# The last sums of a loop pass moved across the loop's branch in a graph network's edge loop

## The chip, the cores and the metric

One Trainium2 chip, one of its eight cores. The metric is the device time of one execution in microseconds, the median of the runs; the profile is of one further execution. All times below are in microseconds unless marked ns.

## What is computed

A graph network of three layers over 3125 nodes and 100000 undirected edges (each is used in both directions), 128 features a node and 16 an edge. A layer builds a message for every edge direction from the two end nodes and the edge, sums the messages at each receiving node, and updates the nodes. At the end stands a layer norm.

```python
def _L0_gnn_ref(nf, ef, src, dst, We1, We2, Wn1, Wn2):
    N, E, D, EF, L = (3125, 12500, 128, 16, 3)
    s2 = jnp.concatenate([src, dst])
    d2 = jnp.concatenate([dst, src])
    ef2 = jnp.concatenate([ef, ef], axis=0)
    h_prev = nf
    for l in range(L):
        e_in = jnp.concatenate([h_prev[s2], h_prev[d2], ef2], axis=-1)
        msg = jax.nn.leaky_relu(e_in @ We1[l]) @ We2[l]
        red = jax.ops.segment_sum(msg, d2, num_segments=N)
        n_in = jnp.concatenate([h_prev, red], axis=-1)
        out = jax.nn.leaky_relu(n_in @ Wn1[l]) @ Wn2[l]
        h_prev = out + h_prev
    return out
...
x = _layernorm(x + _L0_gnn_ref(x, edge_attr_16, src, dst, ...), axis=-1)
```

## The kernel before

**What is done once.** Edges are sorted into buckets by the pair of node blocks (of 128 nodes each; there are 25 blocks) that they join, and cut into tiles of 128 edges that lie in one bucket. For each tile two block numbers are kept, as byte offsets of the blocks: in the array `map_row`, of which a row holds 12 words, the offsets of the 6 tiles of two steps.

**The edge loop.** A step handles three tiles (`STEP`). TensorE does two things in it. *Gathers:* for each tile it multiplies the edge features by their weights (`features`, line 1446, one matmul) and adds the rows of the two end nodes, picked from a table of node features by one-hot matrices `gsel` (`gather`, line 1453, four matmuls, high and low halves). Tile 0 of a step goes to the accumulator `gath6`, a part of `sums`; tiles 1 and 2 go to `gath`. *Sums:* it adds the messages of three steps earlier (`LAG`) to the sums of their nodes (line 1514, 12 matmuls of 128x128, high and low halves, with one-hot matrices `ssel`). The place in `sums` is taken from the offsets.

Between these stand the other engines. ScalarE copies `gath6` to `msg` (line 837), then clears `gath6` (line 840), copies `gath` to `msg` (line 842), and makes the high half of the message of the step before (line 846). The vector engine applies the leaky relu (line 1179) and makes the low half (line 1199). SP issues the loads of `gsel`, `ssel` and the edge features a part (three steps) ahead; in layers 1 and 2 they come from memory, where layer 0 has put them.

**The waits of TensorE in a step**, in order, each on the semaphore named: the part's features and `gsel` (first step of a part alone); `x_set` of the step before (line 842 has emptied `gath`), ahead of the second tile; `ssel` of the part before and `mlo_set`, ahead of the third; and ahead of the sums `gath6_free` (line 840 has cleared `gath6`). `sum_done` is raised at the end of the sums; ScalarE waits for it at line 846 and SP ahead of its loads.

**The loops.** 12 steps are a turn (`STEPS`), and the number of turns, `live_n`, is found at run time. ScalarE, the vector engine and SP loop over 31 turns, of which those from `live_n` on are empty. TensorE loops over 16 passes of two turns, 24 steps: `with pe.If(it * 2 < live_n)` takes the first turn, and an inner `If` the second. Its code for a pass is written out, so that nothing but the loop's branch, two `If`s and the address arithmetic comes between steps. A hint for the branch is given with the loop (`hint_back_edge=True`).

**The offsets in registers.** In layers 1 and 2 TensorE loads a row of 12 words every second step (`next_row(q)`, called within `step` between gathers and sums). Rows that a pass leaves to the next go to the register sets `kept[2]`, `kept[1]` and `kept[0]` (rows 10, 11 and 12 of the pass: the last two rows of this pass, which the late sums still need, and the first of the next). Row 12 is loaded at step 23, the last of a pass, whole. Sums of a step read the row of three steps earlier.

**The end of a layer.** After its last sums TensorE runs the empty passes, leaves the loop, and in `node(l)` begins to multiply (line 1530) once ScalarE has read the sums out (line 852).

## Time and profile before

| | us |
|---|---|
| median of three runs | 3601.3 |
| lowest, highest of them | 3598.9, 3687.4 |
| the profiled execution, its time | 3590.8 |
| its span | 3589.1 |
| about 0 to 1215: sorting, tables | 1215 |
| about 1215 to 2010: edge loop of layer 0 | 795 |
| 2042.7 to 2774: edge loop of layer 1 | 731 |
| 2810.0 to 3541: edge loop of layer 2 | 731 |

The page gives, for one execution, the busy time of each engine and groups of instructions by line. PE is TensorE's matmuls and PEld its weight loads, which run beside them; DVE is the vector engine, ACT is ScalarE, SPq the queue from which SP issues DMAs. In a timeline a row is one instruction or a few like ones: start, duration, engine, line, what it writes and reads, how many, and in brackets how long the engine stood idle ahead of it and who ended that. "issue" in such brackets, or in the chain of waits, is time in which the engine waited for nothing that the profile shows. Ends of matmuls are modelled, so their starts are the safer mark.

### The profile page before, as it was taken

Reading aid. Unit: us, or ns where it says so; the run is one execution under the profiler, and the core shown is the slowest. Engines: PE = TensorE matmul, PEld = TensorE weight load, DVE = VectorE, ACT = ScalarE, POOL = GpSimd, SP = SyncE. Lnnn points to the kernel's source line nnn. Section 1 sums busy time; section 2 is a strip of 40 time slices with the busy share of each in tenths; the row PEclk is TensorE's granted clock in tenths of the full one; section 3 lists DMA queues with packets and bytes.
Section 4 is the critical chain, followed back from the end, with each engine's and each line's share of the span. In section 5 each row is a group of like instructions: output and inputs, shape, how many; then the busy total and the mean of one; then the engine's idle time right before and its main releaser. Section 6 shows DMA issues by size and latency. Waiting matters only on the chain.

```text
span 3589.1 us, 80534 instructions
## 1 busy us (share of the span) xinstructions
PE 2433.9 (68%) x26761; PEld 2105.1 (59%) x26762; DVE 2739.8 (76%) x3385; ACT 2060.4 (57%) x4138; POOL 799.9 (22%) x870
## 2 busy tenths in 40 slices
PE   5000000000004899999999999999999999999996
PEld 4000000000003678787887788888888788888885
DVE  8956565656554799999999877777777777777776
ACT  4000000000002677777877688888888788888885
POOL 0477777777774100000000100000000100000000
PEclk9555555555556999999999999999999999999998
DMA  8111111111112777777777455555555355555553
GB/s 251 46 45 44 34 45 33 45 32 45 30 22 82 239 245 255 256 251 251 253 253 247 169 195 187 189 194 194 190 185 194 120 189 187 193 195 192 185 192 126
DMA packets 227338, 563.52 MB, mean 157 GB/s; under 512 B 43272, under 2 KB 124238, under 8 KB 227182
## 3 DMA queue, kind: packets, MB, share of 16 engines
q1 hardware_dynamic: 199758, 547.80, 44.5%
q0 software_dynamic: 27552, 15.37, 2.3%
q8 instruction: 15, 0.25, 0.0%
q14 instruction: 13, 0.11, 0.0%
HBM read 413.11 MB, written 150.16 MB: 157 GB/s over the span
## 4 chain that ended last, share of the span: by engine, by line
PE 50%; POOL 19%; issue 15%; DVE 13%; SPq 1%; DMA 1%; ACT 1%; DVEq 0%; another core or an unknown queue 0%; ACTq 0%; POOLq 0%
POOL records L672 19%; PE gath L1453 18%; PE sums L1514 13%; PE sums L1453 9%; PE gath L1446 5%; DVE loop_buf L1199 3%; DVE big L1179 3%; PE sums L1446 2%; DVE loop_buf L1216 2%; DVE gsel L1183 2%; DVE table L1137 1%; DVE table L926 1%; PE sums L1530 0%; DMA nums_d<-numT 0%; PE sums L1531 0%
## 5 line engine op out<-in xcount | busy, mean ns | idle before, releaser
L1179 DVE SCALAR_TENSOR_TENSOR big<-big 128x768 f32<-128x768 f32 (+1 forms) x957 | 908.3, 949 | 372.9 <-ACT big L842 349.6
L1453 PE MATMUL gath<-table,gsel 128*128 x7488 | 1072.5, 273 | 0.0
L1199 DVE TENSOR_TENSOR loop_buf<-big,loop_buf 128x768 f16<-128x768 f32 x936 | 890.1, 951 | 0.0
L672 POOL DMA_INDIRECT records<-rec,rowi x784 | 751.4, 958 | 284.5 <-issue 247.3
L1514 PE MATMUL sums<-loop_buf 128*128 128x128 f16 x11232 | 780.3, 219 | 17.1 <-issue 14.1
L1453 PEld LDWEIGHTS gath<-table,gsel 128*128 128x128 f16 x7488 | 732.7, 98 | 83.8
L846 ACT ACTIVATE loop_buf<-big 128x768 f16<-128x768 f32 x936 | 781.4, 835 | 0.0
L842 ACT ACTIVATE big<-gath 128x512 f32<-128x512 f32 x936 | 559.1, 597 | 271.2 <-PE gath L1453 271.2
L1514 PEld LDWEIGHTS sums<-loop_buf 128*128 128x128 f16 x11232 | 649.8, 98 | 105.6 <-ACT sums L840 35.3
L1339 PE MATMUL sums<-table,fchunk 128*128 128x200 f16 x196 | 37.1, 365 | 877.1 <-DVE found L1031 864.7
L1453 PE MATMUL sums<-table,gsel 128*128 x3744 | 562.6, 273 | 14.2 <-DVE gsel L1183 14.2
L1339 PEld LDWEIGHTS sums<-table,fchunk 128*128 128x128 f16 x196 | 24.6, 136 | 889.3 <-issue 886.8
L782 ACT ACTIVATE rec<-big,sc_ef 128x448 f16 x28 | 18.7, 668 | 881.0 <-DMA records<-rec,rowi 881.0
L1446 PE MATMUL gath<-wst,fchunk 128*128 128x256 f16 x1872 | 510.8, 273 | 0.0
L837 ACT ACTIVATE big<-sums 128x256 f32<-128x256 f32 x936 | 352.3, 376 | 92.8 <-PE sums L1453 92.4
L1453 PEld LDWEIGHTS sums<-table,gsel 128*128 128x128 f16 x3744 | 361.3, 98 | 60.2 <-DVE gsel L1183 28.7
L840 ACT ACTIVATE sums<-iota 128x256 f32<-128x256 f16 x936 | 362.9, 388 | 29.6
L707 POOL TENSOR_SCALAR wcs<-wts,sc_w 128x128 f32<-128x128 f32 x2 | 1.2, 611 | 1581.8 <-DVE sc_w L1121 1581.8
L1446 PE MATMUL sums<-wst,fchunk 128*128 128x256 f16 x936 | 255.7, 273 | 37.3 <-issue 37.3
L1052 DVE SCALAR_TENSOR_TENSOR rowi<-rowb,rowc 128x28 int32<-128x28 int32 x28 | 5.3, 188 | 326.3 <-DMA records<-rec,rowi 326.0
L1446 PEld LDWEIGHTS gath<-wst,fchunk 128*128 128x128 f16 x1872 | 183.0, 98 | 31.7 <-issue 0.2
L1216 DVE TENSOR_TENSOR loop_buf<-numc,iota 128x768 f16<-128x768 f16 x312 | 172.0, 551 | 3.9 <-DMA ssel_d<-loop_buf 0.3
(196 smaller groups left out, 1651.3 us busy)
## 6 DMA issues: line engine op xcount, KB each, us to landing
gsel<-gsel_d SPq DMA_DIRECT2D x208, 576.0 KB, 3.7
loop_buf<-ssel_d SPq DMA_DIRECT2D x208, 576.0 KB, 5.1
numb<-nums_d SPq DMA_DIRECT2D x106, 576.0 KB, 4.6
gsel_d<-gsel SPq DMA_DIRECT2D x104, 576.0 KB, 5.5
ssel_d<-loop_buf SPq DMA_DIRECT2D x104, 576.0 KB, 6.4
fchunk<-feat_d SPq DMA_DIRECT2D x630, 80.0 KB, 4.5
loop_buf<-rows_d SPq DMA_DIRECT2D x28, 896.0 KB
records<-rec,rowi POOLq DMA_INDIRECT x784
```

Source lines behind the costliest of these rows:

```text
L672: pool.indirect_dma_start(out=records[:, :], out_offset=bass.IndirectOffsetOnAxis(ap=rowi[:, h, g:g + 1].bitcast(U32), axis=0), in_=rec[:, ...
L837: act.activation(msg[:, place, 0:2 * D], gath6, ACT.Copy).then_inc(x6_set, 1)
L840: act.activation(gath6, iota[:, 0:2 * D], ACT.Copy, scale=0.0).then_inc(gath6_free, 1)
L842: act.activation(msg[:, place, 2 * D:MSG], gath[:, :], ACT.Copy).then_inc(x_set, 1)
L846: act.activation(m_hi[:, (q - 1) % RING, :], msg[:, (q - 1) % RING, :], ACT.Copy)\
L1179: return dve.scalar_tensor_tensor(m, m, SLOPE, m, ALU.mult, ALU.max)
L1183: dve.tensor_scalar(gsel[:, h, :], numb[:, h, :], part[:, 0:1], None, ALU.is_equal).then_inc(gsel_set[h], DMA)
L1199: dve.tensor_tensor(m_lo[:, place, :], msg[:, place, :], m_hi[:, place, :], ALU.subtract)\
L1216: last = dve.tensor_tensor(ssel[:, t % SLOTS:t % SLOTS + STEP, :, :].rearrange("p t s (e w) -> p (t s) e w", w=2), numc[:, 2 * t:2 * (t + ...
L1446: pe.matmul(uv, fchunk[:, p % PARTS, pair * P:(pair + 1) * P], wst[:, side, :, :].rearrange("p s f -> p (s f)"), start=fresh, stop=False, ...
L1453: return pe.matmul(uv, gsel[:, h, (2 * tc + s) * P:(2 * tc + s + 1) * P], at[n], start=False, stop=n == 3, skip_group_check=True)
L1514: last = pe.matmul(sum_at[i, s], m[:, place, w0:w0 + D], ssel[:, ts, s, :], start=False, stop=False, skip_group_check=True)
```

## The change

`step` is parted into `gathers` and `add_sums`. In layers 1 and 2 the last step of a pass (q = 23) does its gathers alone, then comes the loop's branch. The sums of that step (`add_sums(-1, ...)`) stand at the head of the next pass, inside a new `pe.If(it > 0)`. For the pass behind the last live one there is a new `pe.Else()` of the outer `If`: when `it * 2 < live_n + 1`, it loads 8 words of the row that these sums need and does them there. Since `next_row(23)` is no longer called, row 12 is loaded in two pieces: 8 words at step 22, the other 4 at step 0 of the next pass. Layer 0 is as before, and so are all other engines.

```diff
--- before.py
+++ after.py
@@ -88,7 +88,8 @@
 LAG_LOADS = -(-LAG // LOAD_STEPS)
 STEP_WORDS = 2 * STEP
 LOAD_WORDS = LOAD_STEPS * STEP_WORDS
-assert STEPS % LOAD_STEPS == 0 and LOAD_WORDS % 4 == 0
+FIRST_WORDS = 8
+assert STEPS % LOAD_STEPS == 0 and LOAD_WORDS % 4 == 0 and STEP_WORDS <= FIRST_WORDS < LOAD_WORDS
 SLOPE = 0.01
 DEAD = 1000
 EXP_MASK = 0x7F800000
@@ -1457,15 +1458,13 @@
 
                 return [lowered(row(place, s, half)) for s, place in enumerate(places(t)) for half in range(2)]
 
-            def step(q, places, step0, turn, turn_n, before_sums):
+            def gathers(q, places, step0, turn, turn_n):
 
                 p = q // PART_STEPS
                 h = p % 2
                 t = STEP * q
                 first = q % PART_STEPS == 0
                 uv6, uv7 = gath6, (gath[:, 0:2 * D], gath[:, 2 * D:4 * D])
-                sum_at = {}
-
 
                 rows0 = gather_rows(places, t)
                 x_free = at_least(step0 + (q + AHEAD))
@@ -1481,7 +1480,6 @@
 
 
                 rows1 = gather_rows(places, t + 1)
-                free6 = at_least(step0 + (q + 1))
                 pe.wait_ge(x_set, x_free)
                 features(uv7[0], t + 1, p, True)
                 for n in range(4):
@@ -1498,7 +1496,11 @@
                     last = gather(uv7[1], rows2, t + 2, h, n)
                 last.then_inc(gath7_done, 1)
 
-
+            def add_sums(q, places, step0, before_sums):
+
+                t = STEP * q
+                sum_at = {}
+                free6 = at_least(step0 + (q + 1))
                 for i in range(STEP):
                     at = places(t + i - STEP * LAG)
                     for s in (1, 0):
@@ -1515,6 +1517,11 @@
                                              stop=False, skip_group_check=True)
                 last.then_inc(sum_done, 1)
 
+            def step(q, places, step0, turn, turn_n, before_sums):
+
+                gathers(q, places, step0, turn, turn_n)
+                add_sums(q, places, step0, before_sums)
+
             def load_words(first):
 
                 pe.reg_load(words, word_row[0:1, ds(first, WORDS)])
@@ -1587,9 +1594,9 @@
                 tables(l, l - 1)
                 pe.sem_inc(pe_go, 1)
 
-                def row_words(j, turn_n):
-
-                    return map_row[j % LOADS:j % LOADS + 1, ds((turn_n + 1 + j // LOADS) * LOAD_WORDS, LOAD_WORDS)]
+                def row_words(j, turn_n, first=0, count=LOAD_WORDS):
+
+                    return map_row[j % LOADS:j % LOADS + 1, ds((turn_n + 1 + j // LOADS) * LOAD_WORDS + first, count)]
 
                 def bounded(place):
 
@@ -1618,8 +1625,12 @@
                                     row_words(j, it * 2), engines=(mybir.EngineType.PE,),
                                     min_val=0, max_val=(NB - 1) * NODE_BYTES,
                                     skip_runtime_bounds_check_because="sums of the constant steps over the first buckets")
-                            elif q % LOAD_STEPS == LOAD_STEPS - 1:
+                            elif q % LOAD_STEPS == LOAD_STEPS - 1 and j < 2 * LOADS:
                                 keep_row(j, it * 2)
+                            elif q == 2 * STEPS - LOAD_STEPS:
+                                pe.reg_load(kept[0][0:FIRST_WORDS], row_words(2 * LOADS, it * 2, 0, FIRST_WORDS))
+                            elif q == 0:
+                                pe.reg_load(kept[0][FIRST_WORDS:], row_words(0, it * 2, FIRST_WORDS, LOAD_WORDS - FIRST_WORDS))
 
                         def places_at(t):
 
@@ -1628,14 +1639,30 @@
                                                        for r in kept[-j % (2 * LOADS)]]
                             return [bounded(place) for place in row_at[k:k + 2]]
 
+                        with pe.If(it > 0):
+                            add_sums(-1, places_at, step0, lambda q: None)
                         for q in range(STEPS):
                             step(q, places_at, step0, turn, l * live_n + it * 2, next_row)
                         with pe.If(it * 2 + 1 < live_n):
-                            for q in range(STEPS, 2 * STEPS):
+                            for q in range(STEPS, 2 * STEPS - 1):
                                 step(q, places_at, step0, turn, l * live_n + it * 2, next_row)
+                            gathers(2 * STEPS - 1, places_at, step0, turn, l * live_n + it * 2)
                         with pe.Else():
                             for j in range(-LAG_LOADS, 1):
                                 keep_row(j, 0)
+                    with pe.Else():
+                        with pe.If(it * 2 < live_n + 1):
+                            _, ended = nc.values_load_multi_w_load_instructions(
+                                row_words(-LAG_LOADS, it * 2, 0, FIRST_WORDS), engines=(mybir.EngineType.PE,),
+                                min_val=0, max_val=(NB - 1) * NODE_BYTES,
+                                skip_runtime_bounds_check_because="sums of the constant steps over the first buckets")
+
+                            def ended_at(t):
+
+                                k = 2 * t + LAG_LOADS * LOAD_WORDS
+                                return [bounded(place) for place in ended[k:k + 2]]
+
+                            add_sums(-1, ended_at, l * live_n * STEPS + it * (2 * STEPS), lambda q: None)
                 node(l)
 
             for n in range(YSTEPS):
```

## Rows read from the trace of the kernel before

**Rows 1.** The page: busy us of each engine, share of the span, instructions
```profile
PE 2433.9 (68%) x26761; PEld 2105.1 (59%) x26762; DVE 2739.8 (76%) x3385; ACT 2060.4 (57%) x4138; POOL 799.9 (22%) x870
```

**Rows 2.** The page's costliest groups: ScalarE's copy of gath6, whole span
```profile
L837 ACT ACTIVATE big<-sums 128x256 f32<-128x256 f32 x936 | 352.3, 376 | 92.8 <-PE sums L1453 92.4
```

**Rows 3.** Stretches, one pass: length, busy us by engine, TensorE clock, DMA share, GB/s
```profile
core 0: us, PE busy (x) PEld busy (x) DVE busy (x) ACT busy (x) POOL busy (x), PEclk, DMA share, GB/s
2380.88:2437.14 56.26, 55.55 (x648) 49.83 (x648) 43.83 (x49) 47.86 (x96) 0.00 (x0) 1.00 0.54 191
```

**Rows 4.** Chain of waits, layers 1 and 2: start, us, what
```profile
2098.73 0.79 issue
...
2717.77 0.71 issue
...
2865.55 0.71 issue
...
3484.45 0.71 issue
```

**Rows 5.** Timeline around the branch behind a pass of layer 1
```profile
2433.50 0.60 ACT L842 ACTIVATE big<-gath 128x512 f32<-128x512 f32 x1 [0.29 <-PE gath L1453]
...
2435.13 0.39 ACT L840 ACTIVATE sums<-iota 128x256 f32<-128x256 f16 x1
...
2435.57 0.69 PEld L1514 LDWEIGHTS sums<-loop_buf 128*128 128x128 f16 x12
...
2436.64 0.35 SPq L626 DMA_DIRECT2D gsel<-gsel_d  x1
2437.14 0.10 PEld L1446 LDWEIGHTS sums<-wst,fchunk 128*128 128x128 f16 x1 [0.88 <-issue]
2437.15 0.28 PE L1446 MATMUL sums<-wst,fchunk 128*128 128x256 f16 x1 [0.71 <-issue]
```

**Rows 6.** Timeline in the middle of a pass of layer 1, at the inner If
```profile
2407.88 0.69 PEld L1514 LDWEIGHTS sums<-loop_buf 128*128 128x128 f16 x12
...
2408.53 0.10 PEld L1446 LDWEIGHTS sums<-wst,fchunk 128*128 128x128 f16 x1
...
2408.61 0.83 ACT L846 ACTIVATE loop_buf<-big 128x768 f16<-128x768 f32 x1
...
2409.34 0.38 ACT L837 ACTIVATE big<-sums 128x256 f32<-128x256 f32 x1
```

**Rows 7.** Timeline of PEld, two branches behind passes of layer 0
```profile
1271.09 0.67 PEld L1514 LDWEIGHTS sums<-loop_buf 128*128 128x128 f16 x12 [0.76 <-ACT sums L840]
1273.04 0.10 PEld L1446 LDWEIGHTS sums<-wst,fchunk 128*128 128x128 f16 x1 [1.27 <-issue]
...
1393.91 0.67 PEld L1514 LDWEIGHTS sums<-loop_buf 128*128 128x128 f16 x12 [0.64 <-ACT sums L840]
1395.81 0.10 PEld L1446 LDWEIGHTS sums<-wst,fchunk 128*128 128x128 f16 x1 [1.23 <-issue]
```

**Rows 8.** Timeline at the ends of the edge loops of layers 0 and 1
```profile
2011.79 0.30 PEld L1530 LDWEIGHTS sums<-hT,node_w 128*128 128x128 f32 x2 [2.96 <-issue]
...
2773.16 0.69 PEld L1514 LDWEIGHTS sums<-loop_buf 128*128 128x128 f16 x12
...
2773.89 0.83 ACT L846 ACTIVATE loop_buf<-big 128x768 f16<-128x768 f32 x1
...
2776.65 3.83 ACT L852 ACTIVATE big<-sums,sc 128x512 f32<-128x512 f32 x7 [1.92 <-issue]
2777.39 0.30 PEld L1530 LDWEIGHTS sums<-hT,node_w 128*128 128x128 f32 x2 [3.53 <-ACT big L852]
```

**Rows 9.** DMA view: landing (whole span); queues in one later pass; queues in 2044:2101
```profile
gsel<-gsel_d SPq DMA_DIRECT2D x208, 576.0 KB, 3.7
...
q1 hardware_dynamic: 3584, 10.75, 53.8%
...
q8 instruction: 4, 0.07, 0.4%
```

## The prediction, made before the change was run

> **What bounds the kernel now.** I read the page first: over the whole span TensorE is busy 68% and the vector engine 76% [rows 1]. That average mixes stages, so I looked for the stage that the change touches, layers 1 and 2. ScalarE's copy on line 837 runs once a step and has 936 instances [rows 2]; three layers make 312 steps a layer, 26 turns of 12 steps, so 13 passes of 24 steps, all of them whole, and 12 crossings of the loop's branch a layer. The stretches view of one pass [rows 3] then shows what bounds this stage: of 56.26 us TensorE is busy 55.55, ScalarE 47.9, the vector engine 43.8, and the granted clock is 1.00, the 2.4 GHz level. TensorE sets the pace and has about one hole in a pass.
>
> The chain of waits names the hole. Its long pieces include one "issue" per pass, 12 in each layer, from 0.71 to 0.79 us (the first and the last of both layers stand in [rows 4]). "Issue" means that the engine waited for nothing that the profile shows: its sequencer had not handed it the next instruction. The timeline around one of them [rows 5] puts it between the sums of step 23 and the first feature matmul of the next pass, which is where the loop's branch stands. Sums start every 2.307 us elsewhere (2407.88 in [rows 6] to 2435.57 in [rows 5] is 12 steps in 27.69 us), so 24 steps are 55.38 us and one crossing costs 56.26 - 55.38 = 0.88 us. The reader is to see two things: the hole is short, and all 24 together are 24 x 0.88 = 21.1 us, 0.6% of the time. Nothing that this change does in the loop can gain more than that. 2% is 72 us, and it is also about what a measurement of this kernel can tell from no change.
>
> **Why the branch costs what it costs.** I need to know whether the sequencer is ahead of the engine when it comes to the branch. Layer 0 tells. There the sums before a branch wait for ScalarE's clearing of gath6 for 0.76 us once and 0.64 us another time, and from the sums' first weight load to the first one behind the branch it is 1273.04 - 1271.09 = 1.95 and 1395.81 - 1393.91 = 1.90 us [rows 7]. If the sequencer had run on to the branch during the stall, the longer stall would have shortened what follows; it didn't. So the sequencer is held at a wait that isn't met, and begins the rest only when it is released. In layers 1 and 2 it is the same wait: ScalarE's clearing ends at 2435.13 + 0.39 = 2435.52, the sums' first load stands at 2435.57, the first load behind the branch at 2437.14: 1.57 us [rows 5]. That is s, the issuing of 24 instructions of the sums, plus X, the way over the branch. Mid-pass, 2407.88 to 2408.53 is 0.65 us, the engine's own pace, and contains another 24 issues, the not-taken inner branch and the address arithmetic of the next step [rows 6]. So s is at most 0.65 and X at least 0.92. The sequencer comes to the branch with no lead but the sums, which it issues faster than they run.
>
> **The change part by part.** *The sums go behind the branch.* The order of TensorE's own work stays: gathers of step 23, sums of step 23, gathers of step 0. Only the branch moves ahead of the sums. The wait that then stands last ahead of it is x_set, at the second group of the gathers; ScalarE's copy that meets it ends at 2433.50 + 0.60 = 2434.10 [rows 5], 1.4 us earlier than the clearing. From 2434.15 (0.05 for the release, as above) the sequencer issues 20 instructions (20/24 of s), two address operations F, then X, then the new comparison, D. The waits on mlo_set and ssel_set that lie between are met by then (the vector engine's subtraction that mlo_set asks for belongs two steps back, and these arrays came a part ahead). The sums would be reached at 2434.15 + 0.83 s + 2F + (1.57 - s) + D = 2435.72 - 0.17 s + 2F + D.
>
> The unknowns: s lies between 0 and 0.65; I take 0.45, since 0.65 must also hold a branch and an address operation. F lies between 0 and 0.4 (what is left of the 0.65 after issues and a comparison); I take 0.08, because a step holds three more such operations and shows no hole at all. D: at the end of layer 1 ScalarE starts its last m_hi copy at 2773.89 and its first read of the sums at 2776.65 [rows 8]; between lie five empty turns and the exit, six times a jump and two comparisons in 2.76 us: 0.46 each, so 0.15 for one of the three. D lies between 0 and 0.46; I take 0.15. Together: 2435.72 - 0.08 + 0.16 + 0.15 = 2435.95, 0.38 us behind the 2435.57 of today. The hole shrinks from 0.88 to 0.38, a gain of 0.50 a crossing, 24 x 0.50 = 12.0 us. With all unknowns at the kind end (s 0.65, F and D 0) it is 2435.61, a hole of 0.04 and 20 us; at the other (s 0.1, F 0.4, D 0.25, the halfway of its bounds, as all at once is too much) it is 2436.75, a hole of 1.18 and a loss of 7 us.
>
> The Trainium skill (Advanced Engine Details and Errata, Control Flow Timing) gives a compare-and-branch about 0.108 us. No row here shows one alone; with that in place of my 0.15 the sum would be 24 x 0.04 = 1 us better, by an estimate from that page.
>
> *Does the branch hide behind work already queued?* The mid-pass turn is where ScalarE takes its own back edge: its last copy of a turn starts at 2408.61 and runs to 2409.44, and the first copy of the next turn starts at 2409.34 [rows 6]. It crossed its branch while the engine still worked. That speaks for cover at TensorE too, where the last two groups of gathers, two thirds of 2.307 - 0.65 or 1.1 us of work, are issued after x_set.
>
> *The row load in two pieces.* At step 23 a load of 12 words into registers stood between gathers and sums; now 8 words at step 22 and 4 at step 0. There are such loads at every second step, and the sums keep their pitch with and without them (2.307 us over the 12 steps above), so each hides in the sequencer's time before the clearing is done: 2435.52 against about 2434.75 by the sum above. Cost nothing; left at step 23 it would have stood ahead of the branch and eaten the gain. If its cover were gone it would cost at most the 0.77 us between those two times per pass.
>
> *What waits for the moved sums.* sum_done frees m_hi for ScalarE and lets SP issue the loads of the next part. SP's load goes out at 2436.64 today, 0.5 us ahead of the first gathers [rows 5]; afterwards it would go some 0.35 us behind them, as it does at every other part, and lands 3.7 us later [rows 9] for a use three steps, 6.9 us, on. SP's two loads behind it move as far, with the same room. Nothing.
>
> *The last pass of a layer.* The final sums now need a branch back, a comparison, the new Else and a load of 8 words. Today they start at 2773.16, ScalarE reads the sums at 2776.65, held by its own empty turns, and TensorE begins the node matmuls at 2777.39 [rows 8]. Sums would start near 2773.16 + 0.38 + 0.5 to 1.0, thus end by 2775.3: ahead of ScalarE. But TensorE must then pass two more empty rounds and leave the loop. At layer 0's end it does three in at most 2.96 us [rows 8], two thirds of that is 2.0: ready at about 2777.2, up to 2777.8 at the latest. I charge 0.4 us a layer (0 to 1), 0.8 us. The first pass of a layer has the new comparison and a jump over the sums: 0.15 each, 0.3.
>
> **Sum.** 12.0 - 0.8 - 0.3 = 10.9, 11 us. The profiled execution took 3590.8 us and would take 3579.8. The timed runs stand 10 us above it (median 3601.3), which I carry along: 3601.3 - 11 = 3590.3 us, 0.3% less.
>
> **Rivals.** *The hole moves whole (no change or a hair slower).* If TensorE's sequencer takes the backward branch only when the engine's queue is empty, the 0.88 us stand behind the gathers instead of the sums, plus D and the ends: 24 x 0.15 + 1.1 = 5 us more, 3606. [Rows 7] fit this too, since the sums last equally long in both; the ScalarE rows in [rows 6] speak against it. Chance 0.15.
>
> *The hole goes altogether.* If s is large and F and D small, the branch is done before the clearing: a hole near 0.04, 3601.3 - 20 = 3581. Chance 0.08.
>
> *Slower by over 2%: code loading.* The pass grows by the copies of the sums at its head and in the Else. If the head's code then had to be brought in at every crossing, each would wait for a transfer. The nearest row is the 3.7 us to landing of gsel [rows 9]: 24 x 3.7 = 89 us, 3690; it decides from 3.0 us a crossing on (72 us). For it: the first pass of layer 1 shows 4 instruction packets. Against it: a later pass shows only the queue of SP's loads and no instruction packet [rows 9], so the code stays on the chip, and the growth is small. Chance 0.05, of which 0.02 beyond 2%. [...]
>
> **How the numbers follow.** The forecast (gain of 3 to 20 us) has 0.72; the rivals 0.15, 0.08 and 0.05. The range 3578 to 3608 takes in both ends of the unknown costs, the whole-hole rival and the vanished hole, and 2 us for the spread of runs (lowest 3598.9, median 3601.3); outside stays code loading. Faster by over 2% is excluded by the 21.1 us that there are (0.01 for surprise), slower by over 2% 0.03, within 2% 0.96.
>
> **What would show it.** In the profile after: the "issue" wait ahead of line 1446 is gone, and a shorter one, 0.2 to 0.6 us, stands ahead of the sums at the pass's head; a pass takes 55.8 us (55.4 if the hole is gone, 56.4 if it moved whole); the first feature matmul follows those sums at 0.65 us; SP's load goes out behind the first gathers; the node matmuls of a layer begin at most 1 us later relative to ScalarE's copy; no instruction packets in a later pass. The step most likely to be wrong is the lead of the sequencer: F and s are not seen alone in any row.

## Result, and the profile after

The changed kernel took 3580.4 us (median of 4 runs, 3578.0 to 3583.0) beside 3600.1 us before (the mean of 3598.9 and 3601.3): 0.9945 of the time, with a 95% interval of 0.9922 to 0.9969, or a gain of 20 us with an interval of 11 to 28. In some executions of any of these kernels the stages ahead of layer 0 take some 86 us longer; such executions are left out of every time and ratio below, and as the profiles of e4, e8, e9, e10 and e12 are of such ones, I read stretches of layers in them and not the total. The forecast was 3590.3 us, 0.9969, a gain of 11. The time is inside the range and within 2%; the forecast gain lies at the low end of what was measured. The two profiled executions differ by 10.5 us (3590.8 and 3580.3). A later comparison with more runs (e2) gives 14 us. So the size was missed, low, and the question is which terms of the sum were wrong.

First, one pass of layer 1 in the stretches view of the kernel after, from the sums at one pass's head to the same sums of the next (length, busy us by engine, clock, DMA share, GB/s). It answers to [rows 3].

```profile
2378.01:2433.52 55.51, 55.51 (x649) 49.73 (x648) 43.86 (x49) 47.91 (x96) 0.00 (x0) 1.00 0.55 194
```

The pass went from 56.26 to 55.51 us, and by its modelled ends TensorE is busy throughout. Beside 24 steps at the mid-pass pace (55.38 us), 0.13 of the 0.88 us of one crossing is left; the forecast left 0.38. The timeline around the same branch, of the kernel after, answers to [rows 5]:

```profile
2430.64 0.39 ACT L841 ACTIVATE sums<-iota 128x256 f32<-128x256 f16 x1
...
2431.07 0.69 PEld L1516 LDWEIGHTS sums<-loop_buf 128*128 128x128 f16 x12
...
2431.31 0.60 ACT L843 ACTIVATE big<-gath 128x512 f32<-128x512 f32 x1 [0.28 <-PE gath L1454]
...
2432.94 0.39 ACT L841 ACTIVATE sums<-iota 128x256 f32<-128x256 f16 x1
2432.98 0.60 PE L1454 MATMUL gath<-table,gsel 128*128 x4
2433.52 0.67 PEld L1516 LDWEIGHTS sums<-loop_buf 128*128 128x128 f16 x12 [0.23 <-ACT sums L841]
...
2434.15 0.10 PEld L1447 LDWEIGHTS sums<-wst,fchunk 128*128 128x128 f16 x1
...
2434.57 0.35 SPq L627 DMA_DIRECT2D gsel<-gsel_d  x1
```

Step 22's sums load at 2431.07; 2.307 us later would be 2433.38, and step 23's, behind the branch, stand at 2433.52, 0.14 late. ScalarE's copy that releases x_set ends at 2431.91. With the 0.05 us for a release, the way from there over the branch to the sums is 2433.52 - 2431.96 = 1.56 us, where the forecast's sum gave 1.80. Step 0's features follow the sums at 0.63 us, and SP's load goes out 0.42 us behind them, both as foretold. The wait's name in the row (ScalarE's clearing, line 841) needs care: the clearing ended at 2433.33, 0.19 ahead of the load, while in mid-pass a load follows it by 0.04 us (2430.64 + 0.39 = 2431.03, and 2431.07). The sequencer was what came last.

**TensorE's sequencer, row by row.** The trace also holds the register, load and branch instructions of TensorE's sequencer (shown as PEldq when a source line is asked for). These are the arithmetic for step 0 in the kernel before (two of its three instructions) and, of the kernel after, the new comparison and the two instructions with the moved sums' addresses: how many, shortest, median and longest in ns, and when.

```profile
L1433 PEldq FUSED_REGOPS  x1: 148/148/148, 2436.6 to 2436.6; - x1
L1439 PEldq FUSED_REGOPS  x1: 168/168/168, 2436.8 to 2436.8; - x1
```
```profile
L1642 PEldq COMPARE_BRANCH  x1: 71/71/71, 2433.1 to 2433.1; - x1
L1440 PEldq FUSED_REGOPS  x1: 168/168/168, 2433.2 to 2433.2; - x1
L1434 PEldq FUSED_REGOPS  x1: 51/51/51, 2433.4 to 2433.4; - x1
```

From start to start, such an instruction mostly takes its own time and 0.058 to 0.061 us more. With the starts to the nanosecond, as the trace file has them, the way divides so:

| TensorE's sequencer, us | before | after |
|---|---|---|
| addresses of step 23's third tile | ahead of the clearing | 0.15 |
| from the jump behind the inner `If` over the branch to the end of the first comparison | 1.00 (2435.62 to 2436.62) | 0.95 (2432.11 to 2433.07) |
| the new comparison | | 0.13 |
| addresses of the sums | ahead of the clearing | 0.33 (2433.20 to 2433.52) |
| addresses and wait values of step 0 | 0.52 (2436.62 to 2437.14) | behind the moved sums |

The parts of 0.52 and 0.33 are the same, within 0.001, at every crossing but the very first of before (0.59); the way over the branch is 0.95 to 1.00 everywhere but at the first crossing of after's layer 2 (1.06). Two more readings: in the kernel before, the jump starts at 2435.62, 0.10 us after the clearing's end, so all 24 instructions of the sums are handed over in 0.10 us or less; and in after the jump starts at 2432.11, while gathers are still queued until 2433.5.

Now both kernels in stretches between ScalarE's read-out of the sums and the first features of a layer. First the kernel before: node and table stages ahead of layers 1 and 2, then layers 1 and 2.

```profile
2010.99:2042.65 31.66, 29.23 (x101) 17.84 (x102) 24.25 (x56) 16.08 (x27) 11.48 (x22) 1.00 0.26 91
2776.65:2809.99 33.34, 30.96 (x101) 18.41 (x102) 24.44 (x56) 16.19 (x27) 11.46 (x22) 0.95 0.07 27
2042.65:2776.65 734.00, 722.51 (x8424) 647.75 (x8424) 570.05 (x624) 622.40 (x1249) 0.00 (x0) 1.00 0.54 189
2809.99:3543.23 733.24, 722.16 (x8424) 647.72 (x8424) 570.07 (x624) 622.17 (x1248) 0.00 (x0) 1.00 0.53 189
```

The same four of the kernel after:

```profile
2011.73:2045.55 33.82, 30.93 (x101) 18.43 (x102) 24.43 (x56) 16.09 (x27) 11.48 (x22) 0.95 0.24 84
2769.89:2804.93 35.04, 31.21 (x101) 18.50 (x102) 25.12 (x56) 16.18 (x27) 11.46 (x22) 0.95 0.10 38
2045.55:2769.89 724.34, 721.89 (x8424) 646.40 (x8424) 570.03 (x624) 622.93 (x1249) 0.00 (x0) 1.00 0.55 191
2804.93:3530.89 725.96, 723.55 (x8424) 647.63 (x8424) 569.96 (x624) 622.93 (x1248) 0.00 (x0) 1.00 0.55 191
```

| stretch | before | after | difference |
|---|---|---|---|
| start to layer 0's read-out | 2010.99 | 2011.73 | +0.74 |
| node and tables, then layer 1's first features | 31.66 | 33.82 | +2.16 |
| layer 1 | 734.00 | 724.34 | -9.66 |
| node and tables, then layer 2's first features | 33.34 | 35.04 | +1.70 |
| layer 2 | 733.24 | 725.96 | -7.28 |
| the rest, to the span's end | 45.87 | 47.71 | +1.84 |
| span | 3589.1 | 3578.6 | -10.5 |

The layers gave 16.9 us; 6.4 us came back outside them or in other stretches. About half of that isn't the change's: the first node stage of before happens to stand wholly at a granted clock of 1.00 (2.4 GHz), the three others fell to 1.2 GHz for a moment (0.95 in the mean), and the stage is 1.7 us longer for it. The stage behind layer 2 has such a fall in after (at 3532.6) and none in before, and is 1.84 us longer. Without these two falls the difference of the spans would be some 14 us.

Layer 2 gains 2.4 us less than layer 1: 0.8 because it was shorter before, 1.6 because it is longer after. The first pass shows where the 1.6 lie (kernel after, stretches of 4 us at layer 2's start; then the DMA view of 2784 to 2860):

```profile
2805.00:2809.00 4.00, 4.00 (x29) 3.32 (x30) 0.63 (x1) 2.04 (x4) 0.00 (x0) 0.58 0.01 4
2809.00:2813.00 4.00, 4.00 (x45) 3.54 (x44) 2.83 (x4) 2.83 (x7) 0.00 (x0) 1.00 0.00 0
```
```profile
q8 instruction: 7, 0.11, 0.6%
```

TensorE's first steps of layer 2 ran at a mean clock of 0.58, and the queue of instruction packets, empty there in the kernel before, moved seven (of 16 KB each): code was being brought in again. What of the 1.6 us goes with which of the two is sorted out below.

At a layer's end (kernel after; [rows 8] for before):

```profile
2767.62 0.67 PEld L1516 LDWEIGHTS sums<-loop_buf 128*128 128x128 f16 x12 [1.30 <-issue]
...
2769.89 2.42 ACT L853 ACTIVATE big<-sums,sc 128x512 f32<-128x512 f32 x4 [1.92 <-issue]
2770.65 0.30 PEld L1537 LDWEIGHTS sums<-hT,node_w 128*128 128x128 f32 x2 [2.37 <-ACT big L853]
```

The last sums wait 1.30 us for the sequencer, but the node matmuls stand 0.76 us behind ScalarE's read-out, as before (2777.39 - 2776.65 = 0.74). At a layer's start the first features wait longer; these are the rows of after and, below, of before:

```profile
2045.55 0.10 PEld L1447 LDWEIGHTS sums<-wst,fchunk 128*128 128x128 f16 x1 [2.05 <-issue]
```
```profile
2042.65 0.10 PEld L1446 LDWEIGHTS sums<-wst,fchunk 128*128 128x128 f16 x1 [1.58 <-issue]
```

### The profile page after: what moved, and what is told of

Same layout as the page of the kernel before. It is cut to its first block, busy times and chain, and to the rows that moved or that the text cites. A ratio compares the mean times of both kernels' runs of the same rounds, so it can differ in the third digit from the quotient of the medians.

```text
span 3578.6 us, 80654 instructions
## 1 busy us (share of the span) xinstructions
PE 2436.7 (68%) x26761; PEld 2103.2 (59%) x26762; DVE 2741.3 (77%) x3385; ACT 2062.6 (58%) x4138; POOL 800.0 (22%) x870
## 4 chain that ended last, share of the span: by engine, by line
PE 50%; POOL 19%; DVE 15%; issue 13%; DMA 1%; SPq 1%; ACT 1%; DVEq 0%; another core or an unknown queue 0%; ACTq 0%; POOLq 0%
POOL records L673 19%; PE gath L1454 18%; PE sums L1516 14%; PE sums L1454 9%; PE gath L1447 5%; DVE loop_buf L1200 3%; DVE big L1180 3%; PE sums L1447 2%; DVE loop_buf L1217 2%; DVE gsel L1184 2%; DVE table L1138 1%; DVE table L927 1%; PE sums L1537 1%; PE sums L1538 1%; DVE gsel L1064 0%
```

## Experiments

Each run stands beside the kernel before on its own chip. From e1 on every kernel has the bounds checks of e1. "The shifted change" is e3; e4 to e8, e11 and e12 are edits of it (e7 and e12 with 48 matmuls that never run in place of 68, and with the words of layer 0 one place further back in their row), e9 and e10 of the kernel before. All edits but the checks and that place are to TensorE's program. A pass is the distance of two like rows.

**Where the code lies, and the size of the gain.** Before and after as they are, and after with a gap. The counts read from memory get ordinary bounds checks in e1 and e2, in both alike:

```diff
-                map_live[0:1, 0:2], engines=(engine,), min_val=1, max_val=TURNS,
-                skip_runtime_bounds_check_because="counted among the turns and batches; the first always counts")
+                map_live[0:1, 0:2], engines=(engine,), min_val=1, max_val=TURNS)
```

e3 is e2 with matmuls that never run, ahead of the layer loop. By a count of the program in blocks of 256 instructions, TensorE's layer loop touches 8 blocks in e1 and e2, and 7 in e3:

```diff
             node(0)
+            with pe.If(live_n > TURNS - 1):
+                for _ in range(68):
+                    pe.matmul(gath[:, 0:P], zeros16[:, 0:P], zeros16[:, 0:P], start=True, stop=True, skip_group_check=True)
```

> The kernel before with one edit: the two counts of live turns are checked against their bounds when they are loaded, once per engine, a few more instructions (TensorE's program grows by 4). It is the base for the next runs. Theory (the edit is free where it stands): ratio to before 1.000 within 0.002; a pass of layers 1 and 2 takes 56.26 us. Theory 'code size': in the kernel after, TensorE's code was brought in again in layer 2 (9 instruction packets from 2784 to 2857 us, 1 in the kernel before); by a count of the program's instructions in blocks of 256 the layers' loop ended just short of a block's end before (14.99) and lies 0.01 over it here, so this run should show the packets of layer 2 again, and 2 to 4 us in layer 2 that the kernel before does not have. Rival: the packets come from the new Else and If alone, and this run has one packet in layer 2.

> The changed kernel with the same check of bounds. The question is how large the gain is: the profiles say 10.5 us (3589.1 to 3578.6 us of span), the timed runs 20 us. Theory 'crossings': the 24 crossings give 24 x (56.26 - 55.50) = 18.2 us; against it stand about 3 us of reloaded code in layer 2, 0.9 us for the skipped sums at the two first passes, and stretches of halved TensorE clock in the node stages, which come and go between executions (two more in the profile after than before, 1.7 us each). So 13 to 15 us faster than e1 on average: ratio to before 0.996. Rival: 20 us, ratio 0.9945, if before has something more to lose. A pass takes 55.50 us, the wait ahead of the sums at a pass's head 0.23 us.

> The changed kernel of e2 with 138 instructions that never run (a branch skips them) put ahead of the loop over layers 1 and 2, so that this loop touches 7 blocks of 256 instructions (9.03 to 15.70) and not 8 (8.49 to 15.16). Theory 'code size': layer 2 shows at most one or two instruction packets, and the run is 2 to 4 us faster than e2 (ratio 0.995 to 0.996). Rival (the reload is hidden, or has another cause): same time as e2 within 1 us, or packets still there.

Beside 3583.7 us before: e1 took 3584.5 us (ratio 1.0005, 0.9996 to 1.0014), e2 3569.3 (0.9962, 0.9950 to 0.9975), e3 3564.1 (0.9952, 0.9939 to 0.9965). The change is worth 14 us there, and with the code moved 17 us by the ratio (20 by the medians); e2's runs are 3566.8 to 3570.8, e3's 3563.3 to 3567.4. Layers 1 and 2 of e2 and, in the second fence, of e3:

```profile
2034.03:2758.91 724.88, 722.41 (x8424) 647.49 (x8424) 569.99 (x624) 622.27 (x1248) 0.00 (x0) 1.00 0.55 191
2793.91:3520.35 726.44, 723.99 (x8424) 648.50 (x8424) 569.93 (x624) 622.28 (x1249) 0.00 (x0) 1.00 0.55 191
```
```profile
2031.74:2756.10 724.36, 721.91 (x8424) 647.45 (x8424) 569.96 (x624) 622.14 (x1248) 0.00 (x0) 1.00 0.56 191
2789.69:3513.95 724.26, 721.90 (x8424) 647.45 (x8424) 569.96 (x624) 622.13 (x1249) 0.00 (x0) 1.00 0.56 191
```

In e3 layer 2 is as short as layer 1, there is no instruction packet in it, and the node and table stage ahead of it is 33.59 us, where e2 has 35.00.

**The same gap in the kernel before.**

> The kernel before (with bounded counts, as e1) and 138 instructions of TensorE that are never run put ahead of the layer loop, so that the layer loop's code spans seven blocks of 256 instructions, not eight. Theory: what e3 gained over e2 (4.8 us) was the reloading of code in layer 2's first pass, which e1 shows too; this one has no instruction packets in layer 2's first pass and is 3 to 5 us faster than before with bounded counts (about 3580 against 3584.5). Rival: the reload costs nothing that can be measured, and e3's gain is the clock's dips falling otherwise; within 1 us of the kernel before.

```profile
2137.56:2871.31 733.75, 722.24 (x8424) 646.64 (x8424) 569.90 (x624) 622.89 (x1249) 0.00 (x0) 1.00 0.55 189
2905.64:3639.20 733.56, 722.17 (x8424) 646.63 (x8424) 569.90 (x624) 622.81 (x1248) 0.00 (x0) 1.00 0.55 189
```

No packets in layer 2, as expected, but layer 2 is no shorter than in e1, which has them:

```profile
2801.11:3534.59 733.48, 722.16 (x8424) 647.71 (x8424) 569.96 (x624) 622.14 (x1249) 0.00 (x0) 1.00 0.55 189
```

So the theory fell, and the transfers by themselves cost before's loop nothing. (e10's three runs, 3591.0, 3595.1 and 3602.4 us beside 3595.9 and 3597.6, are too few to tell.) What costs in the loop is the clock. e7 shows its price without any late packet: a fall to 1.2 GHz in the first steps of its layer 1, none in layer 2, 726.00 and 724.26 us. Late packets in layer 2 stand in after, e1, e2, e9 and e12; four of these five (not e1) have a fall in layer 2's first steps, and none of the nine kernels without late packets has. That the late code makes the fall likelier is borne out so far; by what way is not shown. In the stage ahead of layer 2 the packets come with a cost of their own: with one fall of the clock it takes 33.3 to 33.7 us in the kernels without late packets (before, e3, e4, e6, e7, e8) and 34.5 to 35.1 in the five with them.

**One compare and branch, D.**

```diff
                         with pe.If(it > 0):
-                            add_sums(-1, places_at, step0, lambda q: None)
+                            with pe.If(it > 0):
+                                with pe.If(it > 0):
+                                    with pe.If(it > 0):
+                                        with pe.If(it > 0):
+                                            add_sums(-1, places_at, step0, lambda q: None)
```

> The shifted change once more, with the sums at the front of a pass inside five nested conditions on the pass number where there was one: four more compares and branches, none of them taken in the 24 passes that do these sums. It measures the term D of the forecast (0.15 us for one compare and branch). In the change a pass is 55.50 us, and the summing weights stand at the engine 0.14 us later than the rhythm of 2.31 us would have them (2433.52, after 2431.07), so nothing hides what is added to that way. Theory D: each compare costs 0.10 to 0.15 us, a pass becomes 55.90 to 56.10 us, and the kernel is 10 to 14 us slower than the shifted change (3564.5). Rival F: a compare that is not taken costs under 0.03 us and the forecast's D was the term that was oversized; passes stay at 55.50 to 55.62 us, the kernel within 3 us of the shifted change.

```profile
2358.15 0.67 PEld L1515 LDWEIGHTS sums<-loop_buf 128*128 128x128 f16 x12 [0.81 <-ACT sums L840]
...
2414.24 0.67 PEld L1515 LDWEIGHTS sums<-loop_buf 128*128 128x128 f16 x12 [0.81 <-ACT sums L840]
```

A pass is 56.09 us, the wait ahead of the sums went from 0.24 to 0.81. Four compares cost 56.09 - 55.51 = 0.58 us, 0.145 each. By the sequencer's rows the five comparisons take 0.127 to 0.135 us each from start to start, but for one of 0.19. The forecast's D = 0.15, read off empty turns of ScalarE, was right, and D was not the term that was too large. The kernel took 0.9994 of before's time (0.9983 to 1.0005): four unneeded conditions eat the gain.

**Step 0's address arithmetic ahead of the sums.** The rows, counts and wait values for step 0's first gathers are formed before the `If` and handed to `gathers`:

```diff
+                        ready = front(0, places_at, step0, turn, l * live_n + it * 2)
                         with pe.If(it > 0):
                             add_sums(-1, places_at, step0, lambda q: None)
-                        for q in range(STEPS):
+                        gathers(0, places_at, step0, turn, l * live_n + it * 2, ready)
+                        add_sums(0, places_at, step0, next_row)
+                        for q in range(1, STEPS):
...
```

> The shifted change with the address arithmetic of step 0's first gathers, and its wait values, computed ahead of the moved sums instead of behind them: 14 register operations (two fused instructions and one single) move to the way from the last gathers to the sums; 4 of the sums' own 10 fall away as shared, so 10 more stand there. In the changed kernel these 14 stand behind the sums, where the forecast left them ahead (it carried the way over the branch, X = 1.57 - s, over whole). The four compares measured 0.145 us each (passes of 56.08 us), so the forecast's D of 0.15 held, and with D at that size its sum can give the 1.56 us that were measured only if a part of X has gone. Theory X: a register operation costs about 0.05 us of the sequencer (layer 0's variant lost about 1.96 us for about 39 more of them at its head), so the 14 were 0.7 us of X; here passes of 55.9 to 56.1 us, a wait of 0.6 to 0.8 us ahead of the sums at the head, the kernel 9 to 14 us slower than the shifted change. Rival s: the arithmetic is nearly free and the sums' issue was slower than s = 0.45 assumed; passes of 55.50 to 55.60 us.

```profile
2356.40 0.67 PEld L1525 LDWEIGHTS sums<-loop_buf 128*128 128x128 f16 x12 [0.64 <-ACT sums L840]
...
2412.32 0.67 PEld L1525 LDWEIGHTS sums<-loop_buf 128*128 128x128 f16 x12 [0.64 <-ACT sums L840]
```

55.92 us: 10 more register operations on the way cost 0.41, 0.041 each (three runs, median 3586.8 us, beside 3595.9 and 3597.6). By the rows the 14 operations take 0.52 us, as in before; the sums' own addresses fall from 0.33 to 0.14, and the comparison takes 0.07 more. Theory X holds, at the low end of its size.

**Register operations by themselves.**

```diff
+                        for k in range(12):
+                            pe.reg_add(spare, spare, kept[1][k])
                         with pe.If(it > 0):
```

> The shifted change with 12 more register additions (two fused instructions) at the front of every pass in layers 1 and 2, ahead of the comparison and the moved sums; their result decides only about a matmul at a layer's end that never runs. It measures one register operation by itself. e8 put 10 more of them there and a pass went from 55.50 to 55.92 us: 0.042 us each. Theory: it is the register operations, however many instructions they are fused in; 12 x 0.042 = 0.50, passes of 56.00 us (55.95 to 56.05). Rival: the fused instruction counts (e8 had two more and one single, 0.14 each); two here cost 0.28, passes of 55.78 us.

```profile
2379.29 0.67 PEld L1516 LDWEIGHTS sums<-loop_buf 128*128 128x128 f16 x12 [0.64 <-ACT sums L840]
...
2435.21 0.67 PEld L1516 LDWEIGHTS sums<-loop_buf 128*128 128x128 f16 x12 [0.64 <-ACT sums L840]
```

55.92 us again, 0.41 for 12 operations in two instructions: 0.034 each. It lies between theory (56.00) and rival (55.78), nearer to the theory. The rows show that both count: the two instructions last 0.185 and 0.038 us, and each is followed by 0.058 us, 0.34 in all; another 0.07 is lost in the sums' addresses behind them. Between 0.034 and 0.041 us an operation, with its share of the instruction, is what these two runs bear out. The kernel took 0.9991 of before's time (0.9981 to 1.0002).

**The row load.** e9 is before with the load in two pieces and the sums in place. e6 loads 12 places whole at step 22 (the moved sums kept), e5 loads them whole behind the last gathers:

```diff
                             gathers(2 * STEPS - 1, places_at, step0, turn, l * live_n + it * 2)
+                            keep_row(2 * LOADS, it * 2)
```

> The kernel before with the other half of the change alone: the first row loaded as 8 places at step 22 and 4 at step 0, the sums left ahead of the branch. In before the load of 12 places at step 23 stands between the gathers and the wait for ScalarE's clearing. e5 showed that such a load costs 1.02 us where nothing hides it (56.52 against 55.50 us). Theory: in before it is hidden by the wait for the clearing (0.77 us between the reach of the wait and its release by the forecast's sum) or all but hidden; passes stay at 56.26 us, or lose up to 0.25 us of it (1.02 - 0.77), that is 0 to 6 us in all. Rival: it stood fully on the way; passes of 55.3 to 55.5 us and the whole gain of the change is the load's, not the sums'.

> The shifted change with the first row loaded whole (12 places) at step 22 and nothing loaded at step 0, so it tells what the two pieces are worth. Theory: a load at step 22 stands ahead of a full queue of matmuls either way, and 12 places take as good as the time of 8; passes stay at 55.50 us, within 0.03 us, and the kernel is within 2 us of the shifted change. Rival: a load holds the sequencer for each register (some 0.03 us each); 12 in one place leave the queue dry at step 22, where 8 do not, and the pass is 0.1 to 0.2 us longer (2 to 5 us in all).

> The shifted change with the first row of 12 places loaded in one piece behind the last gathers of a pass, ahead of the branch (no 8 places at step 22, no 4 at step 0). Theory: the front of a pass waits for the loaded registers before it can pass the branch or form the sums' addresses, so the time of one load (about 0.5 us or more: between 55.38 for 24 steps and 56.26 for a pass of before lie 0.88 us in which such a load, a branch and the addresses stand) lies open: passes of 55.9 to 56.2 us, most of the gain of 0.76 us given back, the kernel 10 to 17 us slower than the shifted change. Rival: the load is asynchronous and the four gathers in the queue (0.60 us) cover it; passes of 55.5 to 55.6 us.

The heads of two passes in e9, in e6 and in e5:

```profile
2362.89 0.10 PEld L1446 LDWEIGHTS sums<-wst,fchunk 128*128 128x128 f16 x1 [0.90 <-issue]
...
2419.18 0.10 PEld L1446 LDWEIGHTS sums<-wst,fchunk 128*128 128x128 f16 x1 [0.90 <-issue]
```
```profile
2327.88 0.67 PEld L1515 LDWEIGHTS sums<-loop_buf 128*128 128x128 f16 x12 [0.24 <-ACT sums L840]
...
2383.39 0.67 PEld L1515 LDWEIGHTS sums<-loop_buf 128*128 128x128 f16 x12 [0.24 <-ACT sums L840]
```
```profile
2330.17 0.67 PEld L1515 LDWEIGHTS sums<-loop_buf 128*128 128x128 f16 x12 [1.25 <-issue]
...
2386.69 0.67 PEld L1515 LDWEIGHTS sums<-loop_buf 128*128 128x128 f16 x12 [1.25 <-issue]
```

The split alone does nothing (56.29 us; e10 has the same), and the two pieces are worth nothing against one at step 22 (55.51). By the rows a load of 12 words lasts 0.85 us; of 4, 8 and 16 words, 0.34, 0.59 and 1.1. In the kernel before it ended at 2435.42, 0.10 us ahead of the clearing's end: covered, but only just. What matters is the place: behind the last gathers the load costs 56.52 - 55.51 = 1.01 us a pass (0.85 for itself, the rest its address and the gaps), more than the sums' move gains, and the kernel is slower than before (1.0025, 1.0013 to 1.0037). e6 took 0.9949 (0.9932 to 0.9965).

**The same move in layer 0.** e7 moves the last sums there too, with the words of the next turns loaded at step 22; e12 has that early load and leaves the sums in place.

```diff
+                    with pe.If(it > 0):
+                        add_sums(-1, unpacked, step0, lambda q: None)
...
-                        if q % STEPS == STEPS - 1:
-                            load_words(it * (2 * STEPS) + (q + 1))
+                        if q == 2 * STEPS - 2:
+                            load_words(it * (2 * STEPS) + 2 * STEPS)
```

> The shifted change with the same move made in layer 0: the last sums of a pass at the front of the next, the 16 words of the next turns loaded at step 22 instead of step 23 and one word further back. In layer 0 of before a turn of the loop costs the weights 1.27 us from the summing weights to the next features (1271.09, 1273.04 in the trace of before) where 0.67 us of loading stands between them in mid-pass. Theory: the hole is the sequencer's, as in layers 1 and 2, and the move takes 0.7 to 1.1 us of it at each of 12 crossings: 8 to 13 us faster than the shifted change, about 3551 to 3556 against 3583.7 of before. Rival: VectorE and the DMA bound layer 0 and TensorE waits for them anyway; the hole shrinks and the waits elsewhere in the pass grow, under 3 us.

> Half of e7: in layer 0 the 16 words are loaded at step 22 and one word further back, as in e7, but the last sums of a pass stay ahead of the branch. e7's passes of layer 0 took 63.8 us against 61.45 of before, with two waits for the sequencer of about 2.1 us, at the head sums and at the sums of step 0. Theory arithmetic: the 28 register operations that the moved sums need in layer 0 (10 in layers 1 and 2) are what made e7 slow; here they stand in mid-pass, and a pass takes 61.3 to 61.6 us, as before. Rival load: the early load of 16 words, or the word one further back, costs it; passes of 62.5 us and more with the sums in place.

e7 took 1.0045 of before's time (1.0030 to 1.0059), some 33 us more than e3's gain would have left. Its steps 22 and 23 in one pass of layer 0, then step 22 and the next pass's features of e12:

```profile
1464.17 0.67 PEld L1516 LDWEIGHTS sums<-loop_buf 128*128 128x128 f16 x12 [2.20 <-issue]
...
1468.48 0.67 PEld L1516 LDWEIGHTS sums<-loop_buf 128*128 128x128 f16 x12 [2.11 <-issue]
```
```profile
1483.99 0.67 PEld L1516 LDWEIGHTS sums<-loop_buf 128*128 128x128 f16 x12 [2.17 <-issue]
...
1488.15 0.10 PEld L1447 LDWEIGHTS sums<-wst,fchunk 128*128 128x128 f16 x1 [1.18 <-issue]
```

A pass of layer 0 is 61.41 us in before (two passes from 1271.09 to 1393.91 in [rows 7]), 62.97 in e12 and 63.62 in e7 (medians of twelve). e12's theory fell and its rival held: the early load alone costs 1.6 us a pass, as a hole of 2.17 us at step 22. (The expectation took e7's first long wait for that of the head sums; e12 shows that it is step 22's.) The loads themselves tell why. These are the loads of 16 words in layer 0, in before and then in e12:

```profile
L1520 PEldq TENSOR_LOAD <-word_row x26: 1102/1107/1261, 1239.8 to 2007.0; - x26
```
```profile
L1527 PEldq TENSOR_LOAD <-word_row x26: 1103/1965/3291, 1327.3 to 2110.2; - x26
```

In e12, as in e7, the 13 loads at step 11 last 1.1 to 1.6 us, as before, and the 13 at step 22 last 2.6 us and more, each of them. The 1.5 us by which the load is longer are nearly all of the pass's 1.6. Why the same load lasts longer at step 22 stays open. The moved sums add another 0.65 us, where in layers 1 and 2 they gain 0.76: in layer 0 each place is unpacked from a word, and the head needs 28 register operations ahead of the sums and 16 for the pass, not 10 and none.

## Why the prediction was right, and where it was wrong

**What bounds the stage, and where the hole lies: right.** 0.88 us at each of 24 crossings, and nothing else moved in a pass.

**The sequencer is held at a wait and crosses the branch as soon as it is released, with matmuls still queued: right.** The rival that the hole moves whole (56.4 us a pass) is out at 55.51. The sequencer's rows show the crossing itself, and e4, e8 and e11 show it from the other side: all that is put on that way appears in the pass in full. The time alone wouldn't have told: 3580.4 us is also what the rival of a vanished hole gives (3581). Its condition, a large s with small F and D, is not what is found below.

**The size of the gain, 0.50 a crossing: wrong.** It was 0.75, 18 us over 24 crossings instead of 12. The step that failed is "then X", in the sentence that adds up the way from x_set: X = 1.57 - s was carried over whole. But X of [rows 5] ends at step 0's features, and the register arithmetic that forms step 0's addresses and wait values (14 operations) stands in it: 0.52 us by the sequencer's rows. In the changed kernel it stands behind the moved sums, whose 0.63 us cover it. e8 puts it back ahead of the sums, where it takes 0.52 again, and the pass is longer by 0.41, as the sums' own addresses are then cheaper. Three more terms, against the same rows:

| term | forecast | shown |
|---|---|---|
| issue of 20 instructions, 0.83 s | 0.37 | under 0.01 |
| two address operations, 2F: the third tile's, the sums' | 0.16 | 0.15 + 0.33 |
| X, as carried over | 1.12 | 0.95, without step 0's 0.52 |
| D | 0.15 | 0.13 |
| sum (of unrounded terms) | 1.80 | 1.56 |

So s was far too large (0.45; at most 0.10 is shown), but it all but cancels in the sum (less than 0.08 us). F was too small by 0.31 in all, since mid-pass, from which it was guessed, the arithmetic is covered. The 0.52 too much and the 0.31 too little leave 0.21 of the 0.24 by which the forecast missed. That it missed by no more is in part luck: two errors of opposite sign.

**D: right** (0.15 taken, 0.145 measured). The figure of 0.108 that the forecast cites from the Trainium skill (Advanced Engine Details and Errata, Control Flow Timing) is 0.04 below what e4 measures for a compare that isn't taken; from start to start the rows give 0.13 to 0.14 in most cases, 0.19 once in e4 and 0.20 in e8. Where the jump is taken within a layer, it is 0.24 to 0.29.

**The row load costs nothing: right** by e9 and e6; that left at step 23 it would eat the gain, right by e5. Its price without cover was put at 0.77 us at most and is 1.01: the bound was the length of the cover, which says nothing of the load, and the cover itself was taken from a sequencer that reaches the wait at 2434.75, where the load ended at 2435.42.

**The layer's ends: charged 0.8, cost nothing.** The sums came 1.30 us late, within what was foreseen, but ScalarE's read-out comes later still. The layer's starts were charged 0.15 each and cost 0.47 and 0.44 (2.05 and 2.07 us of waiting against 1.58 and 1.63): the sums' code has to be jumped over, not only compared, and that comparison takes 0.31 and 0.47 us in the two layers.

**Code loading: not priced at its real place.** The rival looked for a load at every crossing, which doesn't occur. What occurs is one reload ahead of layer 2 and in its first pass, with some 1.3 us in the stage ahead, and in the pass a fall of the clock worth 1.6 us, which came with it in four kernels of five. So the gains were 18.2 us of crossings, less 0.9 at the starts and about 3 around layer 2: 14.3, and e2 measures 14.4 by its medians. Of the 19.7 us of the first comparison the rest, some 5 us, isn't explained by the traces; its interval (11 to 28 us) holds 14.

## What to carry to other kernels

Where an engine's sequencer is held at a wait ahead of a branch, put the longest work that is already free to go behind the branch, and count what stands between the last release and that work: every compare (0.13 to 0.145 us), every register operation (0.034 to 0.041), every load of registers (0.34 us for 4 words to 1.1 for 16, and its address). Count also what then stands behind it and is covered; that was worth as much here as the branch itself. The same move loses where the moved work's addresses are dear to form, or where it forces a load to another step. And look at where the grown loop's code begins: 138 dead instructions ahead of it were worth 4 to 5 us.

## What the runs showed of the hardware that was not expected

- Between two register or branch instructions of TensorE's sequencer lie mostly 0.058 to 0.061 us beside their own time (before, after, e12). A register operation costs 0.034 to 0.041 us with its share of that (e8, e11), so the 10 to 44 that stand ahead of a dynamic matmul matter as soon as the sequencer has no lead.
- A 12-word load of registers costs 1.01 us where it isn't covered (e5) and nothing at all one step earlier (e6). The load instruction lasts 0.34, 0.59, 0.85 and 1.1 us for 4, 8, 12 and 16 words, but at one place in layer 0 (e7, e12) 2.6 us and more for 16.
- Where the layer loop's code touches 8 blocks, by the count in blocks of 256 instructions, code was brought in again around its second turn (after, e1, e2, e9, e12: 9 packets of 16 KB from the end of layer 1 to the end of layer 2's first pass); where it touches 7, it wasn't (before, e3 to e8, e10, e11: one packet), for loops of 1,670 to 1,710 instructions either way.
- The clock fell to 1.2 GHz for a moment in the node stages of nearly every execution, and in after, e2, e9 and e12 also in layer 2's first steps (in e7 and e12 in layer 1's), right behind the stage in which TensorE waited; such a fall there costs 1.7 us (e7).
